# Decoder block: the step column taken ahead of two quantising operations that read a third operand, with new bank choices and task orders

## The reference, cut to what matters

```python
def _L0_attn_ref(X, Wq, bq, Wk, bk, Wv, bv, Wo, bo):
    ...
    scores = jnp.where(causal[None, None], scores, -jnp.inf)
    attn = jax.nn.softmax(scores.astype(jnp.float32), axis=-1).astype(X.dtype)
    out = jnp.einsum('bhqk,bkhd->bqhd', attn, V).reshape(B, S, D)
    return out @ Wo.T + bo
...
def activation_quant(x):
    s = 127.0 / jnp.max(jnp.abs(x), axis=-1, keepdims=True)
    return jnp.clip(jnp.round(s * x), -128, 127) / s
...
xq = activation_quant(rms_norm(x))
g = jax.nn.silu(ternary_matmul(xq, W_g))
u = ternary_matmul(xq, W_u)
p = g * u
return ternary_matmul(p, W_d)
...
x = _layernorm(x + _L0_attn_ref(x, ...), axis=-1)
x = _layernorm(x + _L0_xattn_ref(x, ctx_1024, ...), axis=-1)
x = _layernorm(x + _L0_ffn_ref(x, ...), axis=-1)
```

## Time and profile before

| | before |
|---|---|
| median of 3 runs | 581.6 us (581.37 to 583.06) |
| the profiled execution: time / span | 582.68 us / 580.9 us |
| PE busy | 550.0 us, 95% |
| DVE busy | 478.7 us, 82% |
| ACT busy | 420.7 us, 72% |
| POOL busy | 381.3 us, 66% |

### The profile page before, as it was taken

How to read it: one execution, slowest core, us unless ns; L and a number is a source line. 1 busy time by engine, 2 the same in 40 slices (tenths; PEclk the granted TensorE clock), 3 DMA queues, 4 the chain that set the end, 5 groups by cost and what they waited for, 6 DMA issues and landing times.

```text
span 580.9 us, 14215 instructions
## 1 busy us (share of the span) xinstructions
PE 550.0 (95%) x5324; PEld 356.2 (61%) x5324; DVE 478.7 (82%) x1252; ACT 420.7 (72%) x789; POOL 381.3 (66%) x409
## 2 busy tenths in 40 slices
PE   5999699899989999999989999989999999999995
PEld 4567466685648655786546664777555665575672
DVE  5987899988798798878798857997899887768775
ACT  6999997755978688775768847875697998344251
POOL 1282654455794979687667966967497898666443
PEclk9999799999999999999998999999999999999999
...
GB/s 303 304 332 186 272 244 261 81 55 91 137 65 183 138 120 181 191 173 93 90 110 160 136 160 100 199 144 87 43 117 164 143 188 178 137 109 37 24 33 36
DMA packets 220516, 84.29 MB, mean 145 GB/s; under 512 B 207008, under 2 KB 211616, under 8 KB 218912
## 3 DMA queue, kind: packets, MB, share of 16 engines
...
...
## 4 chain that ended last, share of the span: by engine, by line
PE 47%; DVE 14%; POOL 4%; ACT 2%; issue 2%; DMA 2%; POOLq 0%; DVEq 0%; ACTq 0%; SPq 0%
PE ps_b L665 17%; PE ps_b L813 15%; PE ps_b L828 11%; DVE ps_b L1086 3%; PE ps_b L757 2%; PE ps_b L721 2%; POOL ph L1275 2%; DVE xq L1179 2%; DVE scaled L1176 2%; DVE bn L1019 1%; DVE rows L1214 1%; DMA x1T<-rhl 1%; DMA oT<-ohl 1%; ACT p L910 1%; POOL rstd L1250 1%
## 5 line engine op out<-in xcount | busy, mean ns | idle before, releaser
L1275 POOL TENSOR_TENSOR ph<-p,ph 128x768 f16<-128x768 f32 (+1 forms) x84 | 152.5, 1821 | 80.5 <-ACT ph L846 43.4
L910 ACT ACTIVATE p<-ps_b,tops 128x128 f32<-128x128 f32 (+3 forms) x256 | 120.2, 550 | 25.4 <-issue 15.3
L1086 DVE CUSTOM_DVE_ANT_0 ps_b<-ps_b,future 128x128 f32<-128x128 f32 (+3 forms) x256 | 117.6, 521 | 9.4 <-PE ps_b L721 9.2
L813 PE MATMUL ps_b<-xqT,sg 128*128 128x256 f16 x1024 | 119.1, 273 | 0.9 <-DVE rows L1214 0.6
L828 PE MATMUL ps_b<-sd,hp 128*128 128x512 fp8e4 x512 | 117.1, 379 | 0.0
L813 PEld LDWEIGHTS ps_b<-xqT,sg 128*128 128x128 fp8e4 x1024 | 98.4, 98 | 19.3 <-issue 1.8
L1271 POOL TENSOR_TENSOR hp<-gt,hp 128x512 f16<-128x512 f32 x64 | 74.1, 1161 | 38.9 <-ACT hp L846 38.7
L665 PE MATMUL ps_b<-xhl,wh 128*128 128x256 f16 x480 | 84.2, 275 | 1.0 <-POOL xhl L1275 0.5
L828 PEld LDWEIGHTS ps_b<-sd,hp 128*128 128x128 f16 x512 | 48.6, 98 | 54.8 <-issue 2.4
L846 ACT ACTIVATE ph<-p 128x768 f16<-128x768 f32 (+1 forms) x72 | 66.2, 926 | 3.5 <-DMA pt<-ph 3.3
L665 PE MATMUL ps_b<-xhl,wl 128*128 128x256 f16 x240 | 65.9, 275 | 0.0
...
## 6 DMA issues: line engine op xcount, KB each, us to landing
...
pt<-ph SPq DMA_TRANSPOSE x84, 4.3
...
```

The source lines that it names most:

```text
L813: ins = pe.matmul(ps[:, a * HALF:(a + 1) * HALF], sg[:, ("gg", "uu").index(name), c, ht * P:(ht + 1) * P], xqT[:, c, :], start=c == 0, sto ...
L910: ins = act.activation(p32[:, n % P32_SLOTS, to:to + keys], ps[:, col:col + keys], ACT.Exp, scale=-1.0, bias=tops[:, s % 2, g, j, qt % 2:q ...
L1086: ins = dve.tensor_tensor_reduce(scores, scores, future[:, S - width:S], EXP_SCALE, 3e38, ALU.add, ALU.min, tops[:, s % 2, g, j, qt % 2:qt ...
L1275: pool.tensor_tensor(out_, in_, hi, ALU.subtract).then_inc(signal, 1)
```

## The change

Three things change. In `quantise` the step column is computed ahead of the two large operations, which are now `scalar_tensor_tensor` with a third operand: a column of SBUF (`levels`) that holds the constant or 127, read 512 times over. Two `memset` fill it at the start, so `CONSTS` is 10. The banks in PE's table are chosen by another rule: a task takes the bank that has been free the longest. And all five orders are new; the same tasks stand in them.

```diff
-CONSTS = 8
+CONSTS = 10
...
+        levels = sb("levels", [P, 2], F32)
...
                 dve.reciprocal(scale, step).then_inc(a_scale.sem, 1)
-                wait(dve, a_scale, s, t + 1)
-                wait_for(dve, wx_lo, 1)
-                dve.tensor_scalar(scaled[:, :], row, scale, MAGIC, ALU.mult, ALU.add).then_inc(a_magic.sem, 1)
-                wait(dve, a_magic, s, t + 1)
-                wait(dve, xqT_out[t], s, 0)
-                dve.tensor_scalar(xq[:, t, :], scaled[:, :], MAGIC, 127.0, ALU.subtract, ALU.min)\
-                   .then_inc(xq_out.sem, 1)
                 wait(dve, ln_rstd[2], s, t + 1)
                 wait(dve, invb_out, s - 1, 0)
                 dve.tensor_scalar(normed, step, root, DSCALE, ALU.mult, ALU.mult).then_inc(a_norm.sem, 1)
+                wait(dve, a_scale, s, t + 1)
+                wait_for(dve, wx_lo, 1)
+                wait_for(dve, consts, CONSTS)
+                magic, limit = (levels[:, i:i + 1].to_broadcast([P, D]) for i in range(2))
+                dve.scalar_tensor_tensor(scaled[:, :], row, scale, magic, ALU.mult, ALU.add).then_inc(a_magic.sem, 1)
+                wait(dve, a_magic, s, t + 1)
+                wait(dve, xqT_out[t], s, 0)
+                dve.scalar_tensor_tensor(xq[:, t, :], scaled[:, :], MAGIC, limit, ALU.subtract, ALU.min)\
+                   .then_inc(xq_out.sem, 1)
                 wait(dve, a_norm, s, t + 1)
...
+                const(pool.memset(levels[:, 0:1], MAGIC))
+                const(pool.memset(levels[:, 1:2], 127.0))
...
 PE_ORDER = """
-qp qk0.0.0@7 qk0.0.1@6 qk0.0.3@4 qk0.0.2@5 mx0.0.0.0@6,7,3,2 cp0.1@1 cp0.0@0 va0.0.0@5 va0.0.1@6 bv@1
+qp qk0.0.0@0 qk0.0.1@1 qk0.0.3@3 qk0.0.2@2 cp0.1@4 mx0.0.0.0@5,6,7,0 cp0.0@1 va0.0.0@2 va0.0.1@3 bv@5
```

More of the change, by code:

```diff
@@ new lines @@
+qk0.1.2@0 qk0.1.3@1 tw0.0.2.0.0@2,4 mx0.0.3.0@7,0,6,3 va0.1.1@5 tw0.0.3.0.0@7,0 pv0.0.2.0@6 pv0.0.2.1@6
+mx0.1.0.0@2,4,3,5 pv0.0.2.2@6 pv0.0.2.3@6 pv0.0.3.0@7 pv0.0.3.1@7 tw0.1.0.0.0@0,1 mx0.1.0.1@2,4,3,6 pv0.0.3.2@7
+pv0.0.3.3@7 tw0.1.0.1.0@5,2 mx0.1.1.0@4,3,7,6 qk1.0.0@0 qk1.0.1@1 mx0.1.1.1@5,2,4,3 pv0.1.0.0@7 pv0.1.0.1@7
+tw0.1.1.0.0@0,6 op0.0.0@1 tw0.1.1.1.0@5,2 op0.0.1@0 mx0.1.2.0@4,6,3,1 qk1.0.2@5 mx0.1.2.1@2,0,4,6 pv0.1.0.2@7
+pv0.1.0.3@7 qk1.0.3@3 tw0.1.2.0.0@1,5 xm0.0.0@2 tw0.1.2.1.0@0,7 pv0.1.1.0@3 mx0.1.3.0@4,1,6,5 pv0.1.1.1@3 pv0.1.1.2@3
@@ new lines @@
+ib1@6 dn0.0.1.3@7 va1.1.1@6 mx1.0.3.0@3,2,5,4 pv1.0.0.1@1 pv1.0.0.2@1 pv1.0.0.3@1 pv1.0.1.0@0 pv1.0.1.1@0 qk1.1.2@7
+qk1.1.3@3 mx1.1.0.0@6,2,1,5 gg0.1.2@4 gg0.1.1@7 gg0.1.0@6 pv1.0.1.2@0 pv1.0.1.3@0 gg0.1.5@2 gg0.1.4@1 uu0.1.0@3
+uu0.1.1@0 uu0.1.3@6 uu0.1.2@7 pv1.0.2.0@5 pv1.0.2.1@5 pv1.0.2.2@5 pv1.0.2.3@5 cp1.0@3 cp1.1@0 gg0.1.3@5 gg0.1.7@3
+en1.0@4 dn0.1.0.0@0 uu0.1.4@7 en1.1@5 pv1.0.3.0@4 gg0.1.6@6 pv1.0.3.1@4 pv1.0.3.2@4 pv1.0.3.3@4 dn0.1.0.1@0 en1.2@1
+uu0.1.7@5 uu0.1.5@7 en1.3@4 uu0.1.6@2 dn0.1.1.0@1 dn0.1.1.1@1 mx1.1.0.1@7,6,4,2 dn0.1.0.2@0 op1.0.0@7
@@ new lines @@
+pv2.0.3.1@4 pv2.0.3.2@4 pv2.0.3.3@4 gg1.1.3@7 gg1.1.1@3 uu1.1.0@0 uu1.1.2@4 uu1.1.1@6 pv2.1.0.0@0 pv2.1.0.1@0
+pv2.1.0.2@0 pv2.1.0.3@0 uu1.1.3@2 gg1.1.4@3 gg1.1.5@6 dn1.1.1.0@0 dn1.1.0.0@1 uu1.1.5@5 uu1.1.4@7 gg1.1.6@4 op2.0.0@2
+op2.0.1@3 dn1.1.0.1@1 gg1.1.7@7 dn1.1.0.2@1 uu1.1.6@6 uu1.1.7@2 mx2.1.1.1@5,3,4,7 dn1.1.1.1@0 dn1.1.1.2@0
+mx2.1.2.0@6,2,5,3 dn1.1.0.3@1 dn1.1.1.3@0 mx2.1.2.1@4,7,6,2 xm2.0.1@5 qk3.0.1@1 pv2.1.1.0@3 mx2.1.3.0@0,4,7,6
+xm2.0.0@2 pv2.1.1.1@3 pv2.1.1.2@3 pv2.1.1.3@3 mx2.1.3.1@0,4,7,2 va3.0.0@6 qk3.0.0@5 qk3.0.2@0 pv2.1.2.0@4 pv2.1.2.1@4
@@ new lines @@
+cp1.0 ga0.1.2 cp1.1 ga0.1.3 hh0.1.2 en1.0 hh0.1.3 ez1.0 ga0.1.4 ta1.0 en1.1 ov1.0.3 ga0.1.5 ez1.1 hh0.1.4 to1.0.0
+ta1.1 to1.0.1 en1.2 ga0.1.6 hh0.1.5 ez1.2 en1.3 ta1.2 hh0.1.6 ez1.3 ta1.3 ga0.1.7 ex1.1.0.4 ex1.1.0.5 ex1.1.0.6
+hi1.1.0.1.0 ex1.1.0.7 hi1.1.0.1.1 hh0.1.7 tx1.0.0 ex1.1.1.0 ex1.1.1.1 ex1.1.1.2 hi1.1.1.0.0 ex1.1.1.3 tx1.0.1
+hi1.1.1.0.1 ex1.1.1.4 ex1.1.1.5 zn0.1.0 hi1.1.1.1.0 ov1.1.0 ex1.1.1.6 ex1.1.1.7 hi1.1.1.1.1 zn0.1.1 ex1.1.2.0
+ex1.1.2.1 qk2.0.0 ex1.1.2.2 ex1.1.2.3 hi1.1.2.0.0 n11.0.0 ex1.1.2.4 ex1.1.2.5 hi1.1.2.0.1 ex1.1.2.6 hi1.1.2.1.0
@@ new lines @@
+ex3.1.3.1 ga2.1.6 ex3.1.3.2 ga2.1.7 ex3.1.3.3 hi3.1.3.0.0 hh2.1.6 hh2.1.7 ov3.1.1 ex3.1.3.4 hi3.1.3.0.1 ex3.1.3.5
+ex3.1.3.6 ex3.1.3.7 hi3.1.3.1.0 hi3.1.3.1.1 n13.0.0 ov3.1.2 n13.0.1 ib6 ov3.1.3 zn2.1.0 to3.1.0 to3.1.1 zn2.1.1
+ga3.0.0 ga3.0.1 hh3.0.0 ga3.0.2 hh3.0.1 hh3.0.2 ga3.0.3 ga3.0.4 tx3.1.0 hh3.0.3 hh3.0.4 tx3.1.1 ga3.0.5 ga3.0.6
+hh3.0.5 ga3.0.7 n13.1.0 hh3.0.6 hh3.0.7 n13.1.1 ib7 ga3.1.0 zn3.0.0 ga3.1.1 zn3.0.1 hh3.1.0 hh3.1.1 ga3.1.2 ga3.1.3
+hh3.1.2 hh3.1.3 ga3.1.4 ga3.1.5 hh3.1.4 hh3.1.5 ga3.1.6 ga3.1.7 hh3.1.6 hh3.1.7
@@ new lines @@
+cs2.0 lo2.0.2.0.1 cs2.1 lo2.0.3.0.0 lo2.0.3.0.1 dn1.0.0 lo2.1.0.0.0 dn1.0.1 lo2.1.0.0.1 lo2.1.0.1.0 lo2.1.0.1.1
+rb2.0.0 lo2.1.1.0.0 ta2.0 lo2.1.1.0.1 to2.0.0 hh1.1.0 hh1.1.1 ta2.1 rb2.0.1 to2.0.1 xs3.0.0 hh1.1.2 hh1.1.3 xs3.0.1
+ta2.2 ta2.3 hh1.1.4 tx2.0.0 hh1.1.5 tx2.0.1 os2.0.0 os2.0.1 hh1.1.6 hh1.1.7 lo2.1.1.1.0 lo2.1.1.1.1 lo2.1.2.0.0
+dn1.1.0 dn1.1.1 lo2.1.2.0.1 lo2.1.2.1.0 lo2.1.2.1.1 xm2.0.0 n12.0.0 xm2.0.1 lo2.1.3.0.0 n12.0.1 lo2.1.3.0.1
+lo2.1.3.1.0 rb2.1.0 rb2.1.1 lo2.1.3.1.1 lo3.0.0.0.0 lo3.0.0.0.1 hh2.0.0 hh2.0.1 to2.1.0 to2.1.1 hh2.0.2 hh2.0.3
```

344 lines of the change are left out of this document (157 added, 187 removed).

## The result

The changed kernel is slower: 590.95 us median of 4 runs (588.99 to 592.62) against 582.33 us (581.37 to 584.47, 4 runs) for before on the same chip, a ratio of 1.0144 with an interval of 1.0109 to 1.0179. The forecast was 578.9 us with a range of 574 to 585: wrong in sign, and outside the range. The profiled execution took 591.89 us, with a span of 590.1.

The account below looks back on a forecast made before the run. PE, busy 550.0 of 580.9 us, was taken as the floor; only its idle time and lower-clock time could change. Terms sum to -3.2, 579.5 from the profiled 582.7; from a base of 582.1, 578.9 us, range 574 to 585.

Parts of the forecast that it names:

- The two operations, +1.6: The two large quantising operations on DVE get longer, 7.4 us over 16 tiles, still waiting behind POOL; +1.6 us reaches the end.
- my upper bound (5.4): Most that the longer quantising operations could add at the end: three quarters of their 7.4 us.
- a stretch that might go (-0.9): The 3.41 us at half clock behind PE's wait at 303.68 cost 1.7 us; even chance to go, -0.9.
- a sign of being wrong: Wrong if PE's idle time isn't 1 to 6 us under 19, or new low-clock stretches stand in the first 60 us.
- The start, +0.9: Bias scaling comes later, ACT's first `qk` 3.4 us later, and `cp` waits for the second low part until 20.1: +0.9 us.
- the bound of 3.4: Upper bound of the start's cost, in us, if ACT's lag stays through its full stretch to 75 us.
- My chain: At the start: ACT splits from 13.2, POOL's low part 1.15, scalings 1.7, giving ACT's first `qk` at 18.4 to 19.0 us.
- The column first, 0: Step column ahead of the large operations: waiting for POOL's `rstd` costs nothing, as it is ready at least 0.7 us earlier.
- 57 to 66 us, -1.6: PE's waits of 1.61 and 4.05 us for banks 5 and 7 go, but ACT is full there: -1.6 us.
- the rival that idle time only moves: Half of the releasers are DVE tasks behind quantising, so the last two terms are 0: 582.8 us, chance 0.25.
- `ib` and the other bank waits, -0.2, -3.0, -0.9: First half-step's `ib` wait goes, -0.2; half of 6.1 us of other bank waits, -3.0; half-clock stretch behind 303.68, -0.9.
- The slower rival, VectorE loses: Longer operations still wait for POOL, delaying DVE's maxima and splits each half-step; banks bring nothing: +4.5, 586.6 us, chance 0.15.

Follow-up runs that it names:

- the pair without the third operand: The changed kernel with both large operations back as two-operand `tensor_scalar`: new start 582.23 us (0.9989 of before), first tasks in before's order 579.95 us (0.9945).
- plain operations, old start: The changed kernel with both large operations back as two-operand `tensor_scalar` and the first tasks of all five orders as in before: 579.95 us, 0.9945 of before.
- the plain operations: The changed kernel with only its two large quantising operations back as two-operand `tensor_scalar` with immediates: 582.23 us, 0.9989 of before.
- The reductions: Four runs adding `tensor_reduce` to quantising: plain operations in new orders 1.0028 (between), 1.0064 (behind); both operations accumulating, two between, 1.0042 (new orders), 0.9987 (before's orders).
- the two accumulating kernels of after: The changed kernel with both large operations as `tensor_scalar` also writing a sum (constant, rounding, limit left out): 0.9906 of before; with two reductions between, 1.0042.
- the long accumulating one: The changed kernel with both large operations as sum-writing `tensor_scalar` (constant, rounding, limit left out) and two `tensor_reduce` between them: 585.01 us, 1.0042 of before.
- the short one: The changed kernel with both large operations as sum-writing `tensor_scalar` (constant, rounding, limit left out), no reductions: 577.79 us, 0.9906 of before.
- with the second operation unhindered: Before's orders and banks, step column first, only the second large operation as sum-writing `tensor_scalar` (limit at 127 left out): 576.68 us, 0.9892 of before.

## Why the prediction was wrong, step by step

The change came out 8.4 us slower (0.0144 of 582.3) and the forecast was 3.2 us faster, a miss of 11.6. The runs split it so: third operand +9.0, new start +2.6 (of the pair without the third operand), column first -3.1, and for new orders and banks together -0.1 (± 1.6; plain operations, old start and column first in the new orders and in the old).

- **The two operations, +1.6, measured +9.0 (7.8 with the old start, 5.7 in the orders of before). This is the step that failed: how much of their longer time reaches the end.** The waits behind POOL stayed, as said. The length was somewhat too small: alone the pair is 0.53 us longer a tile and not 0.46, as the first operation takes 750 ns and not 687, and with their waits the two lines take 36.9 us against 27.9 with the plain operations, 9.0 more where the forecast had 7.4. What went wrong by far more is what I made of it. I counted seven half-steps with 0.46 us each, though a half-step has two tiles, and then took half of that as hidden, because DVE is idle for 18% of the span. The reductions show 0.4 to 0.65 us for each us of work; for the 9.4 us of work by which after exceeds the plain form that is 4 to 6 us, near my upper bound (5.4).

  The rest, 3 to 5 us, is more than length explains, though the 9.0 are known to ± 2.3 only. On the line through the two accumulating kernels of after (block 31.7 us at 0.9906, 41.9 at 1.0042) a block of 44.1 us would give 1.0071; after has 1.0144. What after has and those have not is that DVE holds up POOL: POOL is busy for 389.6 us against 382.8 with the plain operations and 377.8 in the long accumulating one. I had priced only DVE's side of the contention. That POOL's side is this rest is argued; no run held up POOL alone. The clock has a share in it: by the estimate above after loses 10.2 us in the mean and the plain form 7.6, 2.6 more, where the long accumulating kernel loses 0.8 more than the short one.
- **The clock.** The sum had the lower clock only as a stretch that might go (-0.9). It was the other way: PE's 5.2 us of extra busy time in the profiled execution are three new stretches and one longer by 3.41 us, at new waits. Of them I had named only one in the first 60 us as a sign of being wrong; that one came, at 21.10.
- **The start, +0.9, measured +2.6 to +3.8.** Direction right, size off, within the bound of 3.4 or just over it. My chain began 1.8 us early (`bv` waited for its load until 14.97), took POOL's low part at 1.15 us instead of 1.60, and put the lag at PE as 0.9 instead of 2.72.
- **The column first, 0, measured -3.1.** Its `rstd` was in time, as said. I priced the operation by its length and not by the gap that it fills (that the gap is the reason is argued).
- **57 to 66 us, -1.6, nothing by the trace (no run parts it).** Both bank waits went and PE waited as long for other things, 2.75 of 5.59 us for the DMA that turns exponentials and 2.1 for ACT, and the half-clock stretch there is 10.24 us long for 6.83: the rival that idle time only moves.
- **`ib` and the other bank waits, -0.2, -3.0, -0.9, measured -0.1 (± 1.6) with all the rest of orders and banks.** I had seen that at 173, 233 and 380 us DVE was late because a quantising operation had waited for POOL, and still gave half of the waits to the bank rule. The runs in the old orders show whose they were: with the second operation unhindered the waits at 173, 233 and 380 went without any new bank or order, and the one at 303 with the column first.

The slower rival, VectorE loses, had the right mechanism with a chance of 0.15 and was too cheap, at 586.6 us: it lacked the held-up POOL and the new half-clock stretches, and had the start at +0.9.

Open: how the rest of the third operand's cost splits between POOL's lateness and the clock (the 2.6 us above are an estimate, and a lower clock behind a wait may itself come of POOL's lateness), and whether the bank rule brings its 0.2%.
